# Two-batch gated attention with a quantised feed-forward: value products on column halves, feed-forward inside the attention loop

## What is computed

```python
qp = Wq @ instance_norm(layernorm(x)) + bq         # per batch, [64, 512]
kp = Wk @ instance_norm(context) + bk
sp = Ws @ context + bs
attn = softmax(qp.T @ kp, axis=-1)                 # [512, 512]
mean, mean_sq = sp @ attn.T, (sp * sp) @ attn.T
std = sqrt(relu(mean_sq - mean * mean))
x = x + tanh(g_xattn) * (instance_norm(context) * std + mean)
w = (weight_q - 8) * scales + zeros                # 512 x 512, per group of 128
x = x + tanh(g_ffn) * (layernorm(x) @ w.T)
```

## Time and profile before

| | us |
|---|---|
| median of 3 runs | 201.22 |
| their range | 200.82 to 201.68 |
| profiled execution, device time | 201.95 |
| its span in the profile | 200.1 |
| PE busy | 171.7 (86%) |
| DVE busy | 157.0 (78%) |
| ACT busy | 127.1 (64%) |
| POOL busy | 120.9 (60%) |

### The profile page before, as it was taken

One profiled execution on the slowest core, in us unless ns is written; L12 is line 12 of the kernel. 1 busy time (PEld: TensorE's weight loads), 2 busy tenths in 40 slices (PEclk: granted clock), 3 DMA queues, 4 the chain that ended last, 5 costly groups with the idle time before them and its releaser, 6 DMA issues.

```text
span 200.1 us, 2899 instructions
## 1 busy us (share of the span) xinstructions
PE 171.7 (86%) x816; PEld 106.3 (53%) x816; DVE 157.0 (78%) x337; ACT 127.1 (64%) x271; POOL 120.9 (60%) x143
## 2 busy tenths in 40 slices
PE   0359799999799979997997999799979893999993
PEld 0235556564465545554644565465446442787882
DVE  3868798779778976997699769955978687999751
ACT  2336767947776685959486948676594994563510
POOL 2125578458645754784487458685798957598300
PEclk9999999999999999999999999999999999699999
DMA  6247680773078127804760540073000000011322
GB/s 164 92 102 213 139 233 0 176 217 135 18 166 271 73 66 154 305 5 115 186 227 0 139 126 0 6 179 80 0 2 0 3 0 0 3 52 52 126 87 105
DMA packets 10880, 20.09 MB, mean 100 GB/s; under 512 B 1648, under 2 KB 1776, under 8 KB 10864
## 3 DMA queue, kind: packets, MB, share of 16 engines
q1 hardware_dynamic: 10864, 19.90, 35.3%
HBM read 9.67 MB, written 2.10 MB: 59 GB/s over the span
## 4 chain that ended last, share of the span: by engine, by line
PE 45%; DVE 26%; ACT 12%; issue 7%; DMA 3%; POOL 2%; SPq 2%; ACTq 0%; DVEq 0%
PE pv_bank L361 11%; PE score_bank L337 8%; ACT probs L484 6%; DVE neg_max L669 5%; PE turn_bank L348 5%; PE score_bank L438 4%; PE score_bank L439 4%; DVE VAR L693 4%; PE score_bank L442 4%; PE proj_bank L373 3%; DVE CTX L650 3%; DVE VAR L698 2%; ACT VAR L501 2%; DMA params_sb<-in_params 2%; DVE q_lo L663 2%
## 5 line engine op out<-in xcount | busy, mean ns | idle before, releaser
L886 POOL TENSOR_SCALAR probs<-probs,rden 128x512 f32<-128x512 f32 x64 | 56.4, 882 | 35.0 <-DVE rden L675 34.6
L484 ACT ACTIVATE probs<-score_bank,neg_max 128x512 f32<-128x512 f32 x64 | 44.3, 692 | 33.6 <-DVE neg_max L669 30.8
L361 PE MATMUL pv_bank<-probs_t,values 128*128 128x512 f32 x120 | 60.3, 604 | 0.9 <-ACT VAR L501 0.6
L669 DVE TENSOR_REDUCE neg_max<-score_bank 128x1 f32<-128x512 f32 x64 | 43.5, 681 | 20.3 <-PE score_bank L337 20.2
L348 PEld LDWEIGHTS turn_bank<-ident,probs 128*128 128x128 f32 x256 | 29.7, 142 | 26.7 <-issue 18.0
L348 PE MATMUL turn_bank<-ident,probs 128*128 128x128 f32 x256 | 37.6, 279 | 3.2 <-ACT probs_t L492 2.8
L492 ACT COPY probs_t<-turn_bank 128x512 f32<-128x512 f32 x64 | 37.3, 586 | 0.2
L361 PEld LDWEIGHTS pv_bank<-probs_t,values 128*128 128x128 f32 x120 | 19.7, 190 | 13.0 <-issue 12.5
L337 PE MATMUL score_bank<-k_hi,q_hi 64*128 64x512 f32 x32 | 16.6, 518 | 2.6 <-DVE k_lo_swapped L759 2.5
L337 PE MATMUL score_bank<-k_hi_swapped,q_hi_swapped 64*128 64x512 f32 x32 | 16.6, 518 | 0.0
L438 PE MATMUL score_bank<-w_hi,yt_hi 128*128 128x512 f32 x32 | 14.1, 440 | 0.0
(11 more groups left out here) (106 smaller groups left out, 343.1 us busy)
## 6 DMA issues: line engine op xcount, KB each, us to landing
X<-in_x SPq DMA_DIRECT2D x8, 256.0 KB, 3.1
CTX<-in_context SPq DMA_DIRECT2D x8, 256.0 KB, 3.4
q_hi_swapped<-q_hi SPq DMA_DIRECT2D x16, 128.0 KB, 2.3
q_lo_swapped<-q_lo SPq DMA_DIRECT2D x16, 128.0 KB, 2.4
ctx_now<-in_context SPq DMA_DIRECT2D x8, 256.0 KB, 2.6
sz<-in_scales_zeros SPq DMA_DIRECT2D x4, 512.0 KB, 4.9
out<-result SPq DMA_DIRECT2D x8, 256.0 KB, 2.0
k_hi_swapped<-k_hi SPq DMA_DIRECT2D x15, 128.0 KB, 2.4
```

The source lines that it names most:

```text
L361: mm = pe.matmul(sums_bank(t, b)[:, :], values[:, i, b, :, :].rearrange("p a c -> p (a c)"), probs_t[b][:, i, :], start=(i == 0), stop=(i ...
L484: act.activation(probs[c % SBANKS][:, :], score_bank[c % SBANKS][:, :], ACT.Exp, bias=neg_max[:, c:c + 1], accum_out=den[:, c:c + 1]).then ...
L669: dve.tensor_reduce(neg_max[:, c:c + 1], score_bank[c % SBANKS][:, :], AX_X, ALU.max, negate=True).then_inc(max_done, 1)
L886: pool.tensor_scalar(probs[c % SBANKS][:, :], probs[c % SBANKS][:, :], rden[:, c:c + 1], 1.0, ALU.mult, ALU.mult).then_inc(probs_done, 1)
```

## The change

What it does:

- **Value products.** `weigh(u, kind, i)` now takes 64 stationary columns and one kind (means or squares) per matmul. Batch 0 writes partitions 0 to 63 and batch 1 partitions 64 to 127 of the same bank, that is, the two are on column halves of the array. `mean_bank` has both batches' means, `sq_bank` both batches' mean squares. There are 16 such matmuls per tile in 8 calls where there were 8 matmuls of 128 columns. All 8 calls of a tile are made during the next tile, one per chunk, after `turn`.
- **No copies.** `keep_sums`, `MEAN` are gone; `square_mean` (ACT) squares from PSUM, `with_mean` and `variance` (DVE) read PSUM.
- **Scores.** A pair is the same block of both batches, so the halves of `q` and `k` are used where they lie; `swap` and its DMAs are gone. The two chunks of a pair lie in two adjacent banks and `maximum` takes both (2 x 512) in one instruction. `project` from the third tile on writes into those score banks.
- **Context.** `CTX` stays raw, the normalised one goes to `CTXN`, and `ctx_now` is gone. All loads, the weights of the feed-forward too, are issued at the start.
- **Feed-forward in the loop.** Tile t - 3 is fed forward in tile t (chunks 2 to 7); three tiles are left for the end. The square root is `Exp(0.5 * Ln(v))` on ACT, with a second table load right after the Tanh at the start.
- **Splits.** ACT rather than DVE makes `x_hi` and `c_hi`.

```diff
-            def weigh(t, b, i):
+            def weigh(u, kind, i):
...
-                mm = pe.matmul(sums_bank(t, b)[:, :], values[:, i, b, :, :].rearrange("p a c -> p (a c)"),
-                               probs_t[b][:, i, :], start=(i == 0), stop=(i == JC - 1))
+                for b in range(2):
+                    mm = pe.matmul(sums_bank[kind][C * b:C * b + C, :], values[u % 2][:, i, b, kind, :],
+                                   probs_t[u % 2][b][:, i, :], start=(i == 0), stop=(i == JC - 1))
...
             def scores(t, p):
+                if p == 0:
+                    pe.wait_ge(q_lo_done, t + 1)
+                    pe.wait_ge(k_lo_done, t + 1)
+                    if 2 <= t + 1 < TILES:
+                        pe.wait_ge(q_lo_done, t + 2)
+                        pe.wait_ge(k_lo_done, t + 2)
...
+            for t in range(TILES):
+                for c in range(CHUNKS):
+                    if c % 2 == 0:
+                        ahead = c // 2 + 2
+                        if ahead < PAIRS:
+                            scores(t, ahead)
+                        elif t + 1 < TILES:
+                            scores(t + 1, ahead - PAIRS)
+                    turn(t, c)
+                    if t > 0:
+                        weigh(t - 1, c // JC, c % JC)
+                    if c == 2 and t + 2 < TILES:
+                        project(t + 2, 0)
+                        project(t + 2, 1)
+                    if c == 2 and t >= 3:
+                        turn_y(t - 3, CHUNKS * t + 2)
+                    if c == 4:
+                        value_product(t)
+                    if c == 5 and t >= 3:
+                        feed_forward(t - 3, 0)
+                    if c == 6 and t >= 3:
+                        feed_forward(t - 3, 1)
+            for i in range(JC):
+                weigh(TILES - 1, 0, i)
+            turn_y(TILES - 3, CHUNKS * TILES)
+            for i in range(JC):
+                weigh(TILES - 1, 1, i)
+            feed_forward(TILES - 3, 0, 1)
+            turn_y(TILES - 2, CHUNKS * TILES)
+            feed_forward(TILES - 2, 0, 1)
+            turn_y(TILES - 1, CHUNKS * TILES)
+            feed_forward(TILES - 1, 0, 1)
...
+            act.preload_act_table_set("natural_log_exp_and_others")
+            split_hi(0, 0)
...
+                    if c == 3 and t + 2 < TILES:
+                        keep_hi(t + 2, 0)
+                        keep_hi(t + 2, 1)
...
+            statistics(1, 0)
+            statistics(1, 1)
+            keep_lo(0, 0)
+            keep_lo(0, 1)
+            normalise(1, 0)
+            normalise(1, 1)
+            maximum(0, 0)
+            statistics(2, 0)
+            maximum(0, 1)
+            statistics(2, 1)
+            reciprocal(0, 0)
...
+                    if c == 3:
+                        if t >= 3:
+                            keep_y_lo(t - 3)
+                        if t + 2 < TILES:
+                            keep_lo(t + 2, 0)
+                            keep_lo(t + 2, 1)
```

More of the change, by code:

```diff
@@ L568, in _ @@
[L568 to L586 removed]
+                    if c == 4 and t >= 1:
+                        square_mean(t - 1)
```

1010 lines of the change are left out of this document (423 added, 587 removed).

## The result

| | before | after |
|---|---|---|
| median of the runs, us | 201.3 (200.82 to 201.68) | 230.04 (229.64 to 230.57) |
| span of the profiled execution | 200.1 | 227.8 |
| start to the first `turn` | 18.1 | 20.2 |
| first `turn` to the last one's end | 142.8 | 180.5 |
| from there to the end | 39.2 | 27.1 |

The changed kernel takes 1.143 times as long (1.139 to 1.147). It loses 37.7 us in the tile loop and 2.1 in the head, and wins back 12.1 at the end. The sum, 27.7, is the difference of the spans.

What follows compares the result with a forecast made beforehand. PE was taken to set the pace. First `turn` 21.7, tile 0 13, tiles 1 to 7 174, a new wait 7 and the end 25.5 sum to a span of 241.2, 242 us on the median's scale; range 216 to 260.

Steps and rivals of the forecast that it cites:

- 13 + 174 + 7: Loop in us: tile 0 takes 13, PE's work in tiles 1 to 7 174, idle before the scores 7.
- The call of a value product: Weigh call on column halves: staggered passes 1.29 plus 0.35 for shape, 1.64 us, 0.78 more than now; main case 0.50.
- the shape: Changing the array's shape around each weigh call: 0.2 in and 0.2 out, taken as 0.35 us with overlap.
- halves in step with that cost: Rival on weigh calls: halves run together but pay for shape, 1.21 per call, 218 to 222 us; chance 0.18, shared with stagger without shape cost.
- The mark I had set: Test in the profile after: the main case is wrong if `turn` follows a `weigh` call within 1 us.
- The point of 0.90 per call: Break-even price of a weigh call: below 0.90 us the changed kernel is faster, above it slower.
- The wait at the scores: Scores overwriting the projections wait for high and low parts: 1.4 us idle in tiles 1 to 5, 7 us.
- moved, not saved: Feed-forward in the loop adds 3.2 us to tiles 3 to 7; the same PE work is paid there or at the end.
- The old gaps: Some 14 us of the old loop left uncounted; a PE with more to do should partly fill these gaps.
- Head and tile 0: First scores at about 14.5 us, first `turn` at 21.7, not 18.14; tile 0 then takes about 13.
- The end: After tile 7: 9.9 us, then the last tile's chain of 15.4, so 25 to 26, taken as 25.5.
- DVE, ACT, POOL as cover: Per tile ACT 14 to 15 us, DVE about 17, POOL about 15, hidden below PE's 23 to 26.

Runs made afterwards that it cites:

- experiment 8: Changed kernel with later scores and two products a call, both products of batch 0 listed ahead of both of batch 1: 210.54 us, beside 210.91 without that order.
- experiment 6: Changed kernel with 128-column value products (values from wrong rows) and the next tile's first scores moved behind value_product: 209.79 us.
- 7: Changed kernel with the next tile's first scores behind value_product and two blocks per weigh call in every second chunk: 210.91 us.
- experiment 5: One feed-forward matmul in place of twelve in five tiles, in both kernels: changed kernel 216.42 us, 13.6 less; kernel before 202.65 beside 201.75.
- experiment 9: Changed kernel with later scores and two products a call, all tiles' feed-forward moved behind the loop, the statistics chain kept inside: 205.37 us.
- experiment 4: Changed kernel with the second table load behind the first high parts and the first reciprocals ahead of the third tile's statistics: 230.23 us.

## Why the prediction was wrong in its main step, and near in its sum

I forecast 242 (216 to 260), slower; it is 230.0, slower. The loop was to take 13 + 174 + 7 = 194 and took 180.5.

**The call of a value product: the step that failed.** I took 1.64, from passes started one behind the other ("the first pass of batch 1 can't start before it, but beside it") plus 0.35 for the shape. The first part was wrong: pairs start 0.007 to 0.015 us apart, in either order of the list (experiment 8). I had chosen the order of the list as the deciding evidence, over the equal starts of the row halves in the earlier trace rows. The second part was near: 0.24 by experiment 6, 0.24 to 0.32 by 7, 0.30 where two calls follow with one `turn` between. So the call costs 0.86 + 0.24 = 1.10 to 1.16, not 1.64. My rival "halves in step with that cost" named 1.21 per call; it is the nearest to the mechanism, though its 218 to 222 did not come out either. With the measured call in my own sum, 242 - 28.6, I would have forecast 213, below my range. The mark I had set, a `turn` within 1 us of the call, is met to 0.01. The point of 0.90 per call, below which I had the kernel faster, was wrong too: with full-width calls of 0.86 it was at 221.6, and at 209.8 with the wait gone as well. The price of the call decided 7.7 to 10.4 us, and not the sign.

**The wait at the scores: right place, half its size.** Forecast 1.4 in five tiles, 7 us. Measured 1.90, 1.90 and three times 2.62 in tiles 1 to 5, or 11.7, and 2.91 in tile 0: 14.6 in all. I had written that it grows as the call gets shorter, by 0.54 here; that gives 1.9, as in tiles 1 and 2. The 2.62 of the next three came in the tiles with feed-forward, where ACT has one copy more, `yt_hi`, of 0.59, ahead of the low parts. That the copy is the cause is argued; the feed-forward's matmuls are not, since without them (experiment 5) the three gaps are still 2.62. Tile 0 I had in another term. What I had not priced is the clock: 6.8 us behind three of these gaps. Moving the scores was worth 12.5.

**The feed-forward: "moved, not saved" was right in sum and wrong in its reason.** I read that PE was "close to full" at the end, and concluded that the feed-forward paid there. PE was indeed never idle from 170 to 190, but the chain of statistics and powers over DVE, POOL and ACT ran beside it and left only 0.7 us to be had (experiment 5). A busy engine at the end was taken for the only bound. In the loop the feed-forward is worth 13.6, and the end became 12.1 shorter once a part of the chain had moved along with it (with the chain alone in the loop, experiment 9, it is 1.1 shorter). That these two nearly cancel is what I had forecast, but not for this reason.

**The old gaps.** I left out some 14 us that my counting did not explain in the loop of before. PE was idle for 10.7 us there; in the changed loop for 19.9, of which 14.6 is the new wait. So about half of the old idle time is gone, but not as I had said, by more work for PE: 6.8 of the 10.7 was one wait in five tiles, of the second projection for `q_lo` in the one `proj_bank`:

```profile
PE proj_bank L319 <- DVE q_lo L663: 6.8, 5, 1.4
```

The changed kernel has a bank for each projection, so this wait is gone, and the one for `k_lo` ahead of the scores stands in its place. It was this old wait that the new one, 11.7 in five tiles, should have been compared with.

**Head and tile 0.** First `turn` forecast 21.7, measured 20.2, before 18.1. Tile 0 forecast 13, measured 19.4, before 16.1: the largest error in the other direction. The scores came at 13.1, not 14.5: the parameters had landed 0.97 earlier (the cast of the weights starts at 5.23, not 6.20), which hid most of the table load. The edit of experiment 4 moved the scores by 0.75 and the first `turn` not at all. One reading was off by little: the earlier trace rows has 0.68 for the maximum of one chunk, so 1.36 for two, where I wrote 1.3; the wide one took 1.22. In tile 0 PE waits for the exponentials and normalising, and goes at half clock in 26.1 to 29.5 and 33.0 to 36.4.

**The end.** Forecast 25.5, measured 27.1. The half clock from 220.7 to 224.1 cost 1.7 of it; PE's waits there are 3.5 us, hand-overs of the last tile that I had counted.

**DVE, ACT, POOL as cover: right.** DVE 58% (I had said below 70%), and beside `k_lo` PE waited for only 2.0 us from 30 to 190. What I did not see is that the cover is thin once the great wait goes: then ACT's `probs_t` stands next, 3.1 to 5.6 us at `turn`.

**The account by experiments.** From 230.0: scores later, -12.5; two products a call, -6.6; feed-forward to the end, -5.5; 205.4, with 3.6 left to the 201.8 that the kernel before gave beside it. In that rest stand 28 calls by 0.24, or 6.7 by the rows, the long tile 3 and the head, against what reading the sums from PSUM gives. These last are not told apart.

**Why the sum came near.** Of the spans' difference, 241.2 to 227.8 or -13.4, tiles 1 to 7 carry: the calls 56 x (1.64 - 1.13) = -28.6, the wait +4.7 (11.7 for 7), the clock +5.1. Tile 0 adds 6.4 (its wait and its half clock within), the first `turn` -1.5, the end +1.6. Together -12.3. One error of 29 us was covered by four of the other sign: that 230 lies within the range is luck, not a right mechanism.

## What to carry to other kernels

Work taken off engines that don't set the pace buys nothing, and what it costs the one that does is paid in full: before work is moved into a loop, make it light at its old place and time that; if nothing is gained, it is free there for as long as what ran beside it stays. Where small matmuls of another shape stand between wide ones, group them: each call in the other shape had a price of 0.24 to 0.32 us here, and grouping by two was worth 6.6 us. Grouping by four made blocks of 3.65 us in an order of work that then waited in every tile. And put a reader of fresh data behind the work that covers its making: one place later in the list was worth 12.5 us.

## What the runs showed of the chip

- Two column halves of 64 work through their own passes independently: in step at a distance of 0.007 to 0.015 us, even with three passes of one half listed between. I had expected strict order.
- An fp32 product on 64 stationary columns streams as long as on 128, 0.43 to 0.48 us a pass; entering and leaving the shape costs 0.24 to 0.30 in all by the rows (0.23 and 0.32 by the lengths of the tiles in experiments 6 and 7). A page of the Trainium skill, "TensorEngine Tiling (Array Packing)" (Key Properties), says that switching the tiling mode drains TensorE; it gives no price, and these rows do.
- The granted clock fell to half (1.2 GHz) in the middle of a loop with PE busy for 8 to 9 tenths, three times, at or just behind a gap of 2.62 or 2.91 us, for 3.4 or 6.8 us each. In the changed kernel it didn't after the gaps of 1.90, nor after one of 2.62; in other variants it did after gaps of 1.52, 1.77, 1.90 and 1.92. So the length of a gap alone does not tell.
- Less work for PE lowered its clock: the kernel before with the light feed-forward ran from 169.8 to 193.7 us at 1.2 GHz, and full width took the mean clock of the changed kernel from 0.954 to 0.934 in the profiled executions (0.940 to 0.954 over all four before, 0.926 to 0.949 with it).
